# A gated cross-attention block: the mask as a one-row bf16 product, row maxima as single fp16 numbers, and a reordered opening

## What is computed

```
x = x + tanh(g_xattn) * attention(memory=ctx, query=layernorm(x), seq_mask, b)
x = x + tanh(g_ffn)   * ffn(layernorm(x), w_gate, w_up, w_down)

attention: 8 heads of depth 32; K, V = halves of memory
    logits  = (Q * 32 ** -0.5) @ K.T + b + -1e30 * (1 - seq_mask)
    weights = softmax(logits)
    out     = weights @ V
ffn: (silu(x @ wg.T) * (x @ wu.T)) @ wd.T, integer weights times 1/127
```

## Time and profile before

| | us |
|---|---|
| median of three runs (lowest, highest) | 163.39 (163.21, 163.62) |
| the profiled execution, its own time | 163.07 |
| its span, first to last instruction | 161.3 |
| PE busy in the span | 139.9 (87%) |
| DVE busy | 122.9 (76%) |
| ACT busy | 102.8 (64%) |
| POOL busy | 91.1 (56%) |
| transfers, mean over the span | 49 GB/s, nearly all in the first 20 us |

### The profile page before, as it was taken

One profiled execution on the slowest core, in us unless ns is written; L12 is line 12 of the kernel. 1 busy time (PEld: TensorE's weight loads), 2 busy tenths in 40 slices (PEclk: granted clock), 3 DMA queues, 4 the chain that ended last, 5 costly groups with the idle time before them and its releaser, 6 DMA issues.

```text
span 161.3 us, 4203 instructions
## 1 busy us (share of the span) xinstructions
PE 139.9 (87%) x1459; PEld 106.6 (66%) x1459; DVE 122.9 (76%) x348; ACT 102.8 (64%) x215; POOL 91.1 (56%) x139
## 2 busy tenths in 40 slices
PE   0768689958796999999999999999999998899970
PEld 0245557735476787968796879687877857676850
DVE  4887899999997878997899689557944856775731
ACT  4327689967556786767675777666767645466530
POOL 6343360542854694689465946644675578784530
PEclk9999999999999999999999999999999999999998
DMA  4699900000000000010002000100020010010022
GB/s 111 195 358 380 326 4 0 6 0 0 0 4 0 6 0 0 6 65 0 4 0 69 2 0 4 65 6 0 0 69 0 0 65 6 0 65 4 0 71 73
DMA packets 7257, 7.92 MB, mean 49 GB/s; under 512 B 816, under 2 KB 6464, under 8 KB 7232
## 3 DMA queue, kind: packets, MB, share of 16 engines
q1 hardware_dynamic: 7056, 7.34, 13.7%
q10 hardware_dynamic: 176, 0.27, 0.6%
HBM read 5.51 MB, written 2.10 MB: 47 GB/s over the span
## 4 chain that ended last, share of the span: by engine, by line
PE 65%; DVE 21%; issue 6%; POOL 2%; DMA 2%; ACT 2%; POOLq 0%; DVEq 0%; ACTq 0%
PE ps L1305 21%; PE ps L1327 10%; PE ps L1123 4%; PE ps L1237 4%; DVE neg_max L991 4%; PE ps L1243 4%; PE ps L1214 3%; PE ps L1216 3%; PE ps L1184 3%; PE ps L1187 3%; PE ps L1257 3%; PE ps L1277 2%; DVE stats L883 2%; DVE gated L1040 2%; DMA x_sb<-in_x_dram 2%
## 5 line engine op out<-in xcount | busy, mean ns | idle before, releaser
L1305 PE MATMUL ps<-n_t,w_gu_t 128*128 128x256 f16 x384 | 49.9, 273 | 1.1 <-DVE h L1051 0.9
L1305 PEld LDWEIGHTS ps<-n_t,w_gu_t 128*128 128x128 f16 x384 | 36.2, 98 | 10.7 <-ACT n_t L786 2.5
L667 POOL TENSOR_TENSOR h<-h 128x256 f16<-128x256 f32 x48 | 32.2, 672 | 16.8 <-ACT h L804 16.2
L795 ACT ACTIVATE tanh_h<-ps 128x256 f32<-128x256 f32 x48 | 18.4, 384 | 17.4 <-PE ps L1305 17.3
L1327 PE MATMUL ps<-w_d_t,h 128*128 128x256 f16 x192 | 28.3, 272 | 0.8 <-DVE x_sb L862 0.4
L991 DVE TENSOR_REDUCE neg_max<-ps 128x4 f32<-128x512 f32 x32 | 21.5, 686 | 8.3 <-PE ps L1187 7.9
L1040 DVE SCALAR_TENSOR_TENSOR gated<-tanh_h,ps 128x256 f32<-128x256 f32 x48 | 19.8, 412 | 6.7 <-ACT tanh_h L795 6.7
L621 POOL TENSOR_TENSOR rstd<-var_eps,neg_half 128x2 f32<-128x2 f32 x16 | 11.1, 697 | 21.8 <-DVE var_eps L890 21.7
L804 ACT ACTIVATE h<-h 128x256 f16<-128x256 f32 x48 | 20.0, 417 | 5.2 <-DVE h L1051 5.1
L748 ACT ACTIVATE probs<-ps,key_bias 128x512 f32<-128x512 f32 x32 | 22.0, 686 | 0.4 <-PE ps L1216 0.4
L1051 DVE SCALAR_TENSOR_TENSOR h<-ps,gated 128x256 f32<-128x256 f32 x48 | 20.4, 424 | 1.7
(11 more groups left out here) (97 smaller groups left out, 221.9 us busy)
## 6 DMA issues: line engine op xcount, KB each, us to landing
x_sb<-in_x_dram SPq DMA_DIRECT2D x8, 256.0 KB, 8.6
out_dram<-x_sb SPq DMA_DIRECT2D x8, 256.0 KB, 2.1
kv<-in_ctx_dram SPq DMA_DIRECT2D x3, 256.0 KB, 8.3
w_raw<-in_L_ffn_w_gate_dram SPq DMA_DIRECT2D x1, 768.0 KB, 6.8
w_raw<-in_L_ffn_w_up_dram SPq DMA_DIRECT2D x1, 768.0 KB, 8.5
w_raw<-in_L_ffn_w_down_dram SPq DMA_DIRECT2D x1, 768.0 KB, 8.4
kv<-in_ctx_dram ACTq DMA_DIRECT2D x1, 256.0 KB, 3.9
mask_raw<-in_mask_BxS_ik_dram ACTq DMA_DIRECT2D x1, 8.0 KB, 2.3
```

Of the source, the lines that this page charges most:

```text
L667: pool.tensor_tensor(h16[:, r % 2, m, 1, :], h32[:, n % NHB, :], h16[:, r % 2, m, 0, :], ALU.subtract).then_inc(h_low, 1)
L1305: ins = pe.matmul(dst, lhs, rhs, start=(w == 0 and (k, l) == terms[0]), stop=(k, l) == terms[-1], skip_group_check=True)
```

## The change

- The mask of the last 128 keys of each batch is loaded as a row into one partition (`mask_row`, first on ACT's queue; the full mask now comes third, behind the first keys). One DVE instruction makes `bias_row` of it, 0 where the key takes part and -42496 where not, in bf16.
- In `row_max` the mask's product multiplies one row of ones by this row: one row of the array where there were 128.
- The row maxima are free of attn_b. DVE's reduction writes them, negated, as fp16 straight into `max_cols16`; the steps of `max_split` are gone from the narrow list. The transposition, ACT's copy and the selector are fp16. The selector is made at the start in fp16 and made again in bf16 for the wide branch.
- ACT's exponential takes a bias for each batch from `exp_bias`, 0 or about -1e30, made by one small instruction in `mask_t` and two in `exp_bias` (behind the first two row maxima).
- The first keys' low part is made by DVE (`k_rest`) and no longer by POOL. The keys' clip is at 7500 and no longer 60000, and the clip of the first keys stands ahead of the first norm.
- SP asks for the gates behind the second x and the second keys.
- `mask_parts` and `mask_rows` have left the opening; `warm_up` is PE's first step; the second `q_stack` copy, `mask_t` and the first `squares` step have moved.
- DVE zeroes one more tile (`max_cols16`) at the very start.

```diff
@@ -54,7 +54,8 @@
-K_LIMIT = 60000.0
+K_LIMIT = 7500.0
+SHUT_OUT = -42496.0
@@ -140,11 +141,11 @@
-    steps = [("stats", 1, 0), ("mask_t",), ("warm_up",), ("norm1", 0), ("high", 1, 0), ("low", 1, 0), ("k_parts", 0),
-             ("mask_parts",), ("mask_rows",), ("dup", 0), ("stats", 1, 1), ("q_stack", 0, 0), ("k_stack", 0),
-             ("norm1", 1), ("q_stack", 0, 1), ("high", 1, 1), ("low", 1, 1), *maxima(0)[:3], ("dup", 1),
-             *maxima(0)[3:], sq(0), ("q_stack", 0, 2), ("max_split", 0), ("max_t", 0), ("q_stack", 0, 3),
-             ("k_parts", 1), ("stats", 1, 2)]
+    steps = [("bias_row",), ("stats", 1, 0), ("warm_up",), ("k_parts", 0), ("norm1", 0), ("k_rest", 0),
+             ("high", 1, 0), ("low", 1, 0), ("mask_cast",), ("dup", 0), ("k_stack", 0), ("stats", 1, 1),
+             ("q_stack", 0, 0), ("q_stack", 0, 1), ("mask_t",), ("norm1", 1), ("high", 1, 1), ("low", 1, 1),
+             *maxima(0)[:2], ("exp_bias",), maxima(0)[2], ("dup", 1), *maxima(0)[3:], ("q_stack", 0, 2),
+             ("max_t", 0), sq(0), ("q_stack", 0, 3), ("k_parts", 1), ("stats", 1, 2)]
@@ -205,7 +206,6 @@
         chore()
         put(mx[3], when=ahead)
         put(("n_t", r - 2), when=normed)
-        put(("max_split", r + 1), when=ahead)
         scores(2)
         put(("attn_t", pb, 2 * ph), when=done)
         product(n + 2)
@@ -374,6 +374,13 @@
+        mask_row = sb("mask_row", [1, B, P], I32)
+        bias_row = sb("bias_row", [1, B, P], BF16)
+        exp_bias = sb("exp_bias", [P, B], F32)
+        max_cols16 = sb("max_cols16", [P, QT, P], F16)
+        max_rows16 = max_rows[:, :, :].rearrange("p n s -> p (n s)").bitcast(F16).rearrange("p (n s) -> p n s", n=2)
+        last_mask = mask_k[:, :].rearrange("p (b c) -> p b c", c=NC)[:, :, LAST]
+        max_sel16 = kv_rest[:, 0, :].bitcast(F16).rearrange("p (h k) -> p h k", h=NH)
@@ -535,10 +542,10 @@
             load_x(sp, 0)
+            load_x(sp, 1)
+            load_kv(sp, 1)
             for n, g in enumerate((g_xattn, g_ffn, attn_b)):
                 sp.dma_start(gates[:, n:n + 1], g.partition_broadcast(P)).then_inc(gates_loaded, 16)
-            load_x(sp, 1)
-            load_kv(sp, 1)
             load_x(sp, 2)
@@ -648,7 +655,7 @@
-                    elif kind == "k_parts":
+                    elif kind == "k_parts" and step[1]:
@@ -677,10 +684,11 @@
+            act.dma_start(mask_row[:, :, :], mask[:, LAST * P:SK].unsqueeze(0)).then_inc(mask_row_loaded, 16)
+            load_kv(act, 0)
             act.dma_start(mask_raw[:, :], mask.rearrange("b (c k) -> (b c) k", k=P)).then_inc(mask_loaded, 16)
-            load_kv(act, 0)
             act.wait_ge(pool_done, CONSTS)
-            act.activation(max_sel[:, :, :], head_rows[:, :].unsqueeze(2).to_broadcast((P, NH, P)), ACT.Copy
+            act.activation(max_sel16[:, :, :], head_rows[:, :].unsqueeze(2).to_broadcast((P, NH, P)), ACT.Copy
                            ).then_inc(selector_ready, 1)
@@ -736,17 +747,22 @@
+                        if is_wide:
+                            act.activation(max_rows[:, n % 2, :], bankb(plan.bank(step))[:, 0:SH],
+                                           ACT.Copy).then_inc(emptied_by["act"], 1)
...
+                            act.activation(max_rows16[:, n % 2, :], bank16(plan.bank(step))[:, 0:SH],
+                                           ACT.Copy).then_inc(emptied_by["act"], 1)
...
-                        act.wait_ge(key_bias_ready, 1)
+                        act.wait_ge(key_bias_ready if is_wide else exp_bias_ready, 1)
...
-                                       bias=key_bias[:, n:n + 1]).then_inc(exp_done, 1)
+                                       bias=key_bias[:, n:n + 1] if is_wide else exp_bias[:, b:b + 1]
+                                       ).then_inc(exp_done, 1)
@@ -825,22 +841,31 @@
-                dve.wait_ge(mask_loaded, 16)
-                dve.tensor_copy(mask_f[:, :], mask_raw[:, :]).then_inc(mask_cast, 1)
                 dve.wait_ge(work_filled, plan.filled(step))
                 dve.tensor_copy(mask_k[:, :], bank32(plan.bank(step))[:, 0:B * NC]).then_inc(emptied_by["dve"], 1)
                 dve.wait_ge(*plan.emptied(step))
+                mine(dve.tensor_scalar(exp_bias[:, :], last_mask, -1.0, 1.0, ALU.mult, ALU.add))
+                mine(dve.tensor_scalar(checks[:, 0:B * NC], mask_k[:, :], 0.0, None, ALU.not_equal))
+                mine(dve.tensor_scalar(checks[:, NZERO:NZERO + B], last_mask, 1.0, None, ALU.is_ge))
+                wait_mine()
+
+                mine(dve.scalar_tensor_tensor(
+                    out=checks[:, 0:B * NC].rearrange("p (b c) -> p b c", c=NC)[:, :, LAST], in0=last_mask, scalar=0.0,
+                    in1=last_mask, op0=ALU.not_equal, op1=ALU.not_equal))
+
+            def exp_bias_steps():
+
+                dve.wait_ge(gates_loaded, 48)
+                mine(dve.tensor_scalar(exp_bias[:, :], exp_bias[:, :], MASK_STEP, gates[:, 2:3], ALU.mult, ALU.add))
+                wait_mine()
+
+                dve.tensor_scalar(exp_bias[:, :], exp_bias[:, :], gates[:, 2:3], 0.0, ALU.subtract, ALU.min
+                                  ).then_inc(exp_bias_ready, 1)
+
+            def mask_parts_steps():
@@ -910,10 +935,26 @@
+                    elif kind == "bias_row":
+
+                        dve.wait_ge(mask_row_loaded, 16)
+                        dve.tensor_scalar(bias_row[:, :, :], mask_row[:, :, :], -SHUT_OUT, SHUT_OUT, ALU.mult, ALU.add
+                                          ).then_inc(bias_row_ready, 1)
+                    elif kind == "mask_cast":
+                        dve.wait_ge(mask_loaded, 16)
+                        dve.tensor_copy(mask_f[:, :], mask_raw[:, :]).then_inc(mask_cast, 1)
                     elif kind == "mask_t":
                         mask_steps(step)
+                    elif kind == "exp_bias":
+                        exp_bias_steps()
                     elif kind == "mask_parts":
                         mask_parts_steps()
+                    elif kind == "k_rest":
+
+                        b = step[1]
+                        dve.wait_ge(k_high, b + 1)
+                        full, high, low = key_parts(b)
+                        dve.tensor_tensor(low, full, high, ALU.subtract).then_inc(k_low, 1)
@@ -981,30 +1022,31 @@
-                            dst = neg_max[:, qt, g * HG:(g + 1) * HG]
+                            if first and h == 0:
+                                dve.wait_ge(zeros_written, 1)
+                            if first and h >= 2:
+                                dve.wait_ge(work_filled, plan.filled(("max_t", h - 2)))
+
+                            dst = max_cols16[:, qt, g * HG:(g + 1) * HG]
@@ -1183,22 +1226,33 @@
-                        rows = bias_rows[:, b * NC + c, :].unsqueeze(1).to_broadcast((P, HG, P))
-                        pe.matmul(bank32(n), ones_b[:, :], rows, start=False, stop=True, skip_group_check=True
+                        if is_wide:
+                            ones, rows = ones_b[:, :], bias_rows[:, b * NC + c, :].unsqueeze(1).to_broadcast((P, HG, P))
+                        else:
+                            pe.wait_ge(bias_row_ready, 1)
+                            ones, rows = ones_b[0:1, :], bias_row[:, b, :].unsqueeze(1).to_broadcast((1, HG, P))
+                        pe.matmul(bank32(n), ones, rows, start=False, stop=True, skip_group_check=True
@@ -1183,22 +1226,33 @@
-                            ins = pe.transpose(bankb(n)[:, t * P:(t + 1) * P],
-                                               max_cols[:, 2 * (step[1] % 2) + t, :], identb[:, :])
+                            at = slice(t * P, (t + 1) * P)
+                            if is_wide:
+                                ins = pe.transpose(bankb(n)[:, at], max_cols[:, 2 * (h % 2) + t, :], identb[:, :])
+                            else:
+                                ins = pe.transpose(bank16(n)[:, at], max_cols16[:, 2 * (h % 2) + t, :], ident16[:, :])
@@ -1213,7 +1267,8 @@
-                            ins = pe.matmul(dst, max_sel[:, h, :], max_rows[:, rows, :], start=False, stop=True,
+                            ins = pe.matmul(dst, (max_sel if is_wide else max_sel16)[:, h, :],
+                                            (max_rows if is_wide else max_rows16)[:, rows, :], start=False, stop=True,
```

More of the change, by code:

```diff
@@ L271, in wide_steps @@
     R = 2 * B
-    steps = []
+    steps = [("mask_parts",)]
     for b in range(B):
@@ L492, in mask_blocks @@
         def mask_blocks(step, table):
-            blocks = table.rearrange("p (b c) k -> p b c k", c=NC)
-            return blocks[:, :, LAST, :] if len(step) == 1 else blocks[:, step[1], :, :]
+            return table.rearrange("p (b c) k -> p b c k", c=NC)[:, step[1], :, :]
         def chunk_kv(b, c):
@@ L701, in run @@
                             act.activation(tanh_g[:, :], gates[:, 0:2], ACT.Tanh).then_inc(tanh_ready, 1)
+                    elif kind == "mask_parts":
```

(27 more changed lines are left out.)

30 lines of the change are left out of this document (12 added, 18 removed).

## The result

| | before | after |
|---|---|---|
| median (lowest, highest), executions | 163.31 (163.21, 163.62), 4 | **170.32** (169.95, 171.14), 4 |
| ratio, 95% interval | | **1.0433** [1.0388, 1.0478] |
| profiled execution, its span | 163.07, 161.3 | 171.14, 169.3 |
| PE, DVE, ACT busy | 139.9, 122.9, 102.8 | 150.4, 117.4, 102.9 |
| start of PE's unbroken stretch | 50.35 | 55.82 |

The kernel became 7.0 us slower; 164.2 was forecast, with 165.8 as the upper end. (Ratios are of executions within 1.5% of a kernel's fastest: they leave out 3 of e2's, 1 of e5's, 6 of e7's, 3 of e11's and 1 of e13's, and e3, with one left, has none; where a kernel falls into two groups, the text gives both.) The last two rows say where the time went: PE's unbroken stretch starts 5.5 us later, where it was forecast 1.8 us earlier, and from there to the end 2.6 us come on top, where 2.5 were forecast.

The account below looks back on a forecast made before the run. DVE and ACT were taken to bound the opening, PE the stretch from 50.4 to 120 us. A lead of 1.8 us, 2.5 us of tile changes and 0.1 for slips gave +0.8: median 164.2 us, range 161.5 to 165.8.

Parts of the forecast that it names:

- the middle: PE-bound stretch from 50.4 to 120 us: 28 tile changes around one-row mask products at 0.09 us each add 2.5 us.
- Rival A: In the middle the one-row product costs no tile change, successor after 0.22 us; median 161.5 us, chance 0.15.
- Some of the products added to PE (below) lie on the way between two reductions, 0.1 to 0.3 us: Opening, up to 50.4 us: added PE work between DVE's reductions takes 0.1 to 0.3 us off the lead.
- rival C: Opening: shared first transfers and 12 mask products at 0.18 us eat the lead down to 0.5; 165.4 us, chance 0.20.
- Nothing lost there: Opening: key clip ahead of the first norm costs nothing, as keys land about 5.1 us while DVE waits for POOL.
- with no one waiting for them: SP's queue in the opening: second x and second keys come earlier, ahead of the gates, at no cost.
- The opening's lead: Up to 50.4 us: first transposition 2.5 us earlier on DVE's path, of which 1.8 us gets through, bounds 0.5 to 3.3.
- ACT as the binding engine: Opening: ACT, busy 11.92 of 12.10 us from 22.2 to 34.3, limits the lead there to 1.9 us.
- rival B: Opening: ACT doesn't bind, so the lead is 3.3 us, with tile changes still costing 2.5; 162.6 us, chance 0.12.

Follow-up runs that it names:

- e2: Changed kernel with the mask's product over 128 rows instead of one, the added rows zero: 162.91 us, 0.9986 of before.
- e5: Kernel before with the mask's product over 64 rows instead of 128: 165.87 us, 1.0146 of before.
- e7: Kernel before with the mask's product over 3 rows in half batches 0 to 3 only: median 167.14 us, in two groups; lower group 1.0044 of before.
- e11: Changed kernel, still one row, with 20 warm-up products instead of 8: median 168.5 us, in two groups; lower group 1.0178 of before.
- e13: e9 with the mask's product over one row everywhere: 165.29 us, 1.0119 of before.
- e3: Changed kernel with the first keys ahead of the mask row on ACT's queue and bias_row behind the first statistics: 169.34 us, 1.037 of before by medians.
- e8: Kernel before with the mask's product over 3 rows in half batches 4 to 7 only: 166.14 us, 1.0183 of before.
- e1: Kernel before with the mask's product over 3 rows instead of 128, everywhere: 170.39 us, 1.0460 of before.
- e4: Edits of e2 and e3 together in the changed kernel: 162.09 us, 0.9948 of before.
- e12: e9 with the first chunk's squares late, behind the max_t step as in the changed kernel: 161.93 us, 0.9882 of before.
- e9: Changed kernel with 128 rows in the mask's product and loads, bias_row step and first squares put back in order: 160.82 us, 0.9868 of before.
- e14: e9 with the mask's product over one row in half batches 4 to 7 only: 163.42 us, 1.0039 of before.
- e10: e9 with 12 warm-up products instead of 8: 161.76 us, 0.9885 of before.

## Why the prediction was wrong

**Direction right, size far off.** Slower was the likeliest outcome, with 0.58; the range ended 4.5 us too low. The direction was in part luck: the term that made it slower, the middle, is 2.6 of the 7.0 us, and the larger rest comes from the opening, which was forecast to be faster.

*The middle, right.* 0.09 us per change of tile, 28 changes, 2.5 us: measured 0.096 in front and 0.101 behind, and next to nothing behind it where a 128x32 tile follows; 2.6 us in the profile, 2.85 in e8. Only the stretch itself was misread: it doesn't last 69.6 us, which is the length of the row's window, but 79.0 (50.35 to 129.37), and 81.5 after (55.82 to 137.30). One pair of instructions over 16 rows had the price. Rival A falls: 0.317 us start to start, not 0.216. Of the Trainium skill's page "TensorEngine Tiling (Array Packing)", Key Properties, "Mode switching requires drain" held in the fast phase too.

*"Some of the products added to PE (below) lie on the way between two reductions, 0.1 to 0.3 us": the step that failed.* This is all that the sum holds for the products over few rows in the opening. They cost 4.25 us (e1 less e8), and in e7 0 to 1 us when the clock comes back by 19.20 and 4 to 5 us more otherwise. The prediction noted that the warm-up ran at 1.2 GHz and then costed every later product at 2.4, because before does so. It never asked what a later or a different PE does to the grant. With the low clock the opening's products take about twice as long; DVE's 15.23 us and ACT's 13.89 of the earlier trace rows stopped being the bound. The 12 x 0.18 us of rival C were priced at the high clock too: 2.2 us of PE work, where the low clock alone costs 4 to 5. Why the clock comes back so late with few rows stays open.

*"Nothing lost there", a second step that failed.* The keys were taken to land at 5.1, because their 3.9 us of the earlier trace rows was carried over to a different order of issues. They landed at 8.30. A strided row of 2 KB held ACT's queue for 1.25 us, and the second x and keys, 512 KB, were in flight from SP's queue ahead of the gates. The prediction wrote that these come earlier "with no one waiting for them"; true of themselves, but they share the engines with the keys, for which by the new order even the norm waits. Rival C named this sharing and gave it, with 12 more costs of 0.18, 1.3 us. e3 shows that with the keys in front somebody else pays: the keys, asked for first, landed after 3.8 us, and the first statistics started at 4.68 instead of 3.53, 2.21 us of it a wait for the first x. With 128 rows the price is 0.8 us for the order on ACT's queue (e2 less e4), 1.7 with SP's order and the place of `bias_row` as well (e2 less e12), and 1.9 with that of the squares too (e2 less e9).

*The opening's lead, right once both are away.* The copy was forecast at 8.3, e9 has 8.55; last maximum's end 15.6, measured 15.97; first transposition 15.65, measured 16.12 (the late q_stacks transpositions now stand before it); ACT's first exponential 18.4, measured 18.26; start of the unbroken stretch 48.6, measured 48.09 (e14), 49.19 (e12), 47.35 (e9). The keys' low part on DVE took 0.69, forecast 0.7; in after the new bias row held the statistics back by 0.16 us (3.69 against 3.53), where the forecast had nothing. DVE lost 5.5 us in all, forecast 6. In after itself none of that was seen: 11.32, 19.07, 19.40, 22.34.

*ACT as the binding engine.* In e9 ACT was busy 15.09 of 16 us from 20 to 36 (DVE 14.84), which speaks for the forecast's limit and against rival B, yet the lead came out at 3.0 in the execution with the best clock. The two aren't told apart, since no two executions here had the same clock in both kernels.

Not tried: what in the products over few rows the grant responds to, a run with the changed order of SP's queue alone, and a profile of an e7 execution in the slow group.

## What to carry to other kernels

Fewer rows in use don't make a product of TensorE cheaper; in a stream of full products, one over 64 rows or fewer costs 0.1 us on each side, so feed zeros into the unused rows (96 and 128 rows cost nothing here). Before moving a load or putting a wait in front of an opening, ask what TensorE does meanwhile and at which clock it comes back: here half the clock made PE the bound, for 4 to 5 us, where late keys alone cost about 1. When an order of issues changes, no landing time of the old order may be carried over, and no step that is ready should be queued behind one that waits for a transfer.

## What the runs showed that was not expected

The same program took 162.89 to 164.38 or 167.01 to 169.13 us (e7), with mean granted clocks of 0.982 to 0.992 and 0.946 to 0.959. The first group's profile has a low stretch from 15.79 to 19.20; that the second group's lasts to about 30 is an estimate from its mean clocks and from e1 and e11, which have such means (0.953 and 0.952) and are low from about 16 to 29.5. With 3 rows everywhere (e1) every execution was as slow as the slow group with the middle's 2.85 us on top; with 96 or 128 rows the longest low stretch behind the first rise in a profiled execution was 6.8 us (e10, e12), at a price of about 1 us. The mean clock of an execution doesn't always tell: where the trace has no record before a late first rise, the low stretch ahead of it isn't counted, and two executions of the changed kernel show 0.993 and 0.994 at 170.0 us. e3's profile is such a case. Its row from 20 to 36 us says 1.00, although the record begins at 28.64 and PE is busy throughout:

```profile
20.00:36.00 16.00, 16.00 (x145) 9.71 (x143) 11.04 (x22) 12.86 (x28) 4.40 (x8) 1.00 0.01 4
```

The start-to-start times of the transpositions (0.056 or 0.107 us) show the clock where the record doesn't.

The issue of a transfer of one partition, 4 pieces of 512 bytes, took 1.25 us on ACT's queue (1.18 and 1.19 in e3 and e9), and the keys' behind it 0.36.
